# Two rounds of solve products with one stationary operand, merged into 256-column products, and two engines that change banks

## The reference, cut to what matters

```
M = where(stril, einsum("bhncd,bhnmd->bhncm", k_beta, k) * decay, 0.0)
T = solve_triangular(eye + M, eye, lower=True)
v_c = einsum("bhnij,bhnjd->bhnid", T, v_beta)
k_cumdecay = einsum("bhnij,bhnjd->bhnid", T, k_beta * exp(g))
```

## Time and profile before

| | |
|---|---|
| median of three runs | 4081.28 us (4079.53 to 4088.25) |
| the profiled execution | 4083.4 us, span 4081.7 us |
| mean granted TensorE clock | 0.967 |
| TensorE busy | 3375.8 us, 83% |
| VectorE busy | 2804.7 us, 69% |
| ScalarE busy | 1829.1 us, 45% |
| GpSimd busy | 1214.0 us, 30% |

### The profile page before, as it was taken

One profiled execution on the slowest core, in us unless ns is written; L12 is line 12 of the kernel. 1 busy time (PEld: TensorE's weight loads), 2 busy tenths in 40 slices (PEclk: granted clock), 3 DMA queues, 4 the chain that ended last, 5 costly groups with the idle time before them and its releaser, 6 DMA issues. The chain is left out here.

```text
span 4081.7 us, 63279 instructions
## 1 busy us (share of the span) xinstructions
PE 3375.8 (83%) x18978; PEld 2667.9 (65%) x18978; DVE 2804.7 (69%) x5764; ACT 1829.1 (45%) x4272; POOL 1214.0 (30%) x2414
## 2 busy tenths in 40 slices
PE   0000379999999999999999999999999999999987
PEld 0000367777777777777777777777777777777763
DVE  6999357676777767676767676767676766767653
ACT  2222145454545554454545454545454554445541
POOL 2222323233232323232323232332333232323210
PEclk9999989999999999999999999999999999999998
DMA  2000412222222222222222221222222221222202
GB/s 88 0 0 0 188 49 65 76 65 71 68 71 61 69 67 55 69 70 71 70 69 70 65 70 50 70 71 65 73 67 70 64 66 50 71 71 71 65 5 93
DMA packets 288110, 262.37 MB, mean 64 GB/s; under 512 B 220896, under 2 KB 249696, under 8 KB 276960
## 3 DMA queue, kind: packets, MB, share of 16 engines
q1 hardware_dynamic: 278528, 123.60, 12.5%
q10 hardware_dynamic: 9216, 134.22, 8.9%
HBM read 228.11 MB, written 29.62 MB: 63 GB/s over the span
## 5 line engine op out<-in xcount | busy, mean ns | idle before, releaser
L575 PE MATMUL x<-xs,w_high 128*128 128x512 f32 x3072 | 1090.2, 437 | 113.0 <-issue 72.3
L575 PEld LDWEIGHTS x<-xs,w_high 128*128 128x128 f32 x3072 | 546.5, 198 | 182.4 <-issue 79.6
L575 PE MATMUL x<-xs,w_low 128*128 128x512 f32 x1536 | 623.9, 406 | 0.0
L810 ACT ACTIVATE uvec<-rb,cpos 128x128 f32<-128x128 f32 x512 | 160.6, 365 | 957.6 <-PE rb L595 957.6
L869 ACT ACTIVATE slot<-lane 128x512 fp32r<-128x512 f32 x640 | 352.7, 609 | 492.7 <-PE lane L701 492.5
L1149 POOL TENSOR_TENSOR block_step<-block_in 64x14 f32<-64x14 f32 (+6 forms) x896 | 228.6, 255 | 497.0 <-DMA block_in<-blocks_dram 377.3
L1179 POOL TENSOR_TENSOR rstd<-rarg,powers 128x8 f32<-128x8 f32 x64 | 105.0, 1640 | 889.0 <-DVE rarg L988 889.0
L366 PE MATMUL gate<-wba,mixed 128*128 128x64 f32 x128 | 27.6, 421 | 413.1 <-DVE nega L328 413.1
L575 PEld LDWEIGHTS x<-xs,w_low 128*128 128x128 f32 x1536 | 300.1, 195 | 70.9
L940 DVE SCALAR_TENSOR_TENSOR cacc<-x,cwqk,cacc 128x511 f32<-128x511 f32 (+2 forms) x384 | 281.3, 746 | 44.0 <-ACT cacc L797 22.8
L940 DVE SCALAR_TENSOR_TENSOR cacc<-x,cwv,cacc 128x511 f32<-128x511 f32 (+2 forms) x384 | 281.8, 748 | 38.6 <-ACT cacc L797 4.2
(11 more groups left out here) (203 smaller groups left out, 7491.5 us busy)
## 6 DMA issues: line engine op xcount, KB each, us to landing
xs<-mix_dram ACTq DMA_DIRECT2D x64, 2048.0 KB, 7.6
gb<-cum_dram SPq DMA_DIRECT2D x128, 256.0 KB, 4.3
w_in<-in_w_qkvz SPq DMA_DIRECT2D x48, 512.0 KB, 4.9
w_out<-in_w_out SPq DMA_DIRECT2D x16, 512.0 KB, 6.1
blocks_dram<-bt SPq DMA_DIRECT2D x512, 8.0 KB, 1.5
inverse_dram<-block_out SPq DMA_DIRECT2D x64, 128.0 KB, 2.2
inv<-inverse_dram SPq DMA_DIRECT2D x512, 16.0 KB, 1.8
xacc<-in_x SPq DMA_DIRECT2D x1, 4096.0 KB, 13.3
```

Source lines behind the costliest of these rows:

```text
L575: ins = mm(PROJ_BANK[kind][i][:, :], w, x, start=(k == 0 and j == 0), stop=(k == KC - 1 and j == 2))
L810: ins = a(uvec[:, h, :], rb[:, sl(h, HD)], ACT.Copy, scale=sm2[p]["cpos"][:, ch, h:h + 1])
```

## The change

Jobs 3 and 4 no longer go head by head and operand by operand. Job 3 makes, for head 0, the products of s0 with both moving operands, turned and s1, in one piece of 256 columns per chunk; job 4 does the same for head 1. Chunks 0 and 1 go to bank 0, chunks 2 and 3 to bank 1 (`shared_product`). For that, s1 moves into inv16 behind turned, and inv16 changes its order of dimensions. Each bank now holds results for both engines: VectorE takes the turned halves into pinv, ScalarE the s1 halves into lower. VectorE begins with bank 0 and ScalarE with bank 1, and each waits for the other before it takes the other bank. Job 5 waits for both engines. The blocks are stored in two DMAs, one for natural and one for turned, the memset of inv16 covers the new part too, and job 10 takes (s2, pinv) in place of (s1, s2).

```diff
-        inv16 = sb("inv16", [P, HPG, NCH, 2, CH], F32R)
+        inv16 = sb("inv16", [P, 3, HPG, NCH, CH], F32R)
-        slot = [sb(f"slot{i}", [P, HPG, NCH, CH], F32R) for i in range(3)]
+        slot = [sb(f"slot{i}", [P, HPG, NCH, CH], F32R) for i in range(2)]
-        ADDED = (4, 6, 7, 9, 10)
+        COPIED = (0, 1, 2, 3, 4, 5, 8)
+        ADDED = (3, 4, 6, 7, 9, 10)
...
-            if k not in ADDED:
-                engine.wait_ge(copied[h], (JOBS - len(ADDED)) * m + sum(1 for i in range(k + 1) if i not in ADDED))
-            else:
+            if k in COPIED:
+                engine.wait_ge(copied[h], len(COPIED) * m + COPIED.index(k) + 1)
+            if k in ADDED:
                 engine.wait_ge(added[h], len(ADDED) * m + ADDED.index(k) + 1)
...
-                sp.dma_start(t["inverse_dram"].rearrange("a q w i j -> (a q) w i j"), block_out[:, :, :, :].bitcast(F32)).then_inc(S["block_stored"], 16)
-                sp.wait_ge(S["block_stored"], m * 16 + 16)
+                for w in range(2):
+                    sp.dma_start(t["inverse_dram"][:, w].rearrange("a q i j -> a q (i j)"), block_out[:, w, :, :].rearrange("q i j -> q (i j)").bitcast(F32)).then_inc(S["block_stored"], 16)
+                sp.wait_ge(S["block_stored"], m * 32 + 32)
...
             PRODUCTS = [
                 (lower, natural),
                 (natural, lower),
                 (s1, s0),
-                (s0, s1),
-                (s0, turned),
+                None,
+                None,
                 (lower, s2),
                 (s2, pinv),
                 (s0, pinv),
                 (pinv, None),
                 (None, s1),
-                (s1, s2),
+                (s2, pinv),
             ]
+
+            def shared_product(m, k):
+                h = k - 3
+                for half in range(2):
+                    await_product(pe, m, half, k - 1)
+                    for j in range(2):
+                        ch = 2 * half + j
+                        ins = mm(lane[half][:, sl(j, 2 * CH)], s0[:, h, ch, :], inv16[:, 1:3, h, ch, :], start=True, stop=True)
+                    ins.then_inc(prod_full[half], 1)
...
+                if (k, h) == (5, 1):
+                    await_product(pe, m, 0, k - 1)
...
-                        for h in range(HPG):
-                            product(m, n, k - FIRST, h, 1 - p)
+                        if k - FIRST in (3, 4):
+                            shared_product(m, k - FIRST)
+                        else:
+                            for h in range(HPG):
+                                product(m, n, k - FIRST, h, 1 - p)
...
-                    if A and job >= 0 and job not in ADDED:
+                    if A and job in (3, 4):
+                        for half in (1, 0):
+                            act.wait_ge(prod_full[half], JOBS * m + job + 1)
+                            if half == 0:
+                                act.wait_ge(added[0], len(ADDED) * m + ADDED.index(job) + 1)
+                            a(lower[:, job - 3, sl(half, 2), :], lane[half][:, :].rearrange("p (c w s) -> p c w s", c=2, w=2)[:, :, 1, :], ACT.Copy).then_inc(copied[half], 1)
+                    elif A and job in COPIED:
...
-                    if job == 4:
-                        ins = v.tensor_tensor(pinv[:, h, :, :], made, turned[:, h, :, :], ALU.add)
+                    if job in (3, 4):
+                        if h == 1:
+                            dve.wait_ge(copied[1], len(COPIED) * m + COPIED.index(job) + 1)
+                        made = lane[h][:, :].rearrange("p (c w s) -> p c w s", c=2, w=2)[:, :, 0, :]
+                        ins = v.tensor_tensor(pinv[:, job - 3, sl(h, 2), :], made, turned[:, job - 3, sl(h, 2), :], ALU.add)
```

More of the change, by code:

```diff
@@ L520, in scatter_blocks @@
                     rows = slice(a * BLK, (a + 1) * BLK)
-                    sp.dma_start(inv16[rows, :, :, :, rows].rearrange("i h c w j -> i (h c w) j").bitcast(F32),
-                                 t["inverse_dram"][a].rearrange("q w i j -> i (q w) j")).then_inc(S["inv16_loaded"], 16)
+                    sp.dma_start(inv16[rows, 0:2, :, :, rows].rearrange("i w h c j -> i (w h c) j").bitcast(F32),
+                                 t["inverse_dram"][a].rearrange("w q i j -> i (w q) j")).then_inc(S["inv16_loaded"], 16)
             def body(l, m, n, b):
@@ L668, in out_half @@
                     ins.then_inc(S["op_full"], 1)
-            s0, s1, s2 = slot
-            natural, turned = inv16[:, :, :, 0, :], inv16[:, :, :, 1, :]
+            s0, s2 = slot
+            natural, s1 = inv16[:, 0, :, :, :], inv16[:, 2, :, :, :]
             RESIDUAL = JOBS - 2
@@ L909, in body @@
                                 load_input((b + 1) % BATCH)
-            s0, s1, s2 = slot
-            DEST = [s0, s1, s2, lower, pinv, s0, pinv, pinv, s1, s2, solve]
+            s0, s2 = slot
+            s1 = inv16[:, 2, :, :, :]
+            DEST = [s0, s1, s2, None, None, s0, None, None, s1]
             LOOP(act, body)
@@ L919, in _ @@
             W = lambda name, x: dve.wait_ge(S[name], x)
-            s0, s1, s2 = slot
-            turned = inv16[:, :, :, 1, :]
+            s0, s2 = slot
+            turned, s1 = inv16[:, 1, :, :, :], inv16[:, 2, :, :, :]
             def v_columns(m):
@@ L1147, in invert_blocks @@
                     if i == BLK - 2 and m is not None:
-                        pool.wait_ge(S["block_stored"], m * 16 + 16)
+                        pool.wait_ge(S["block_stored"], m * 32 + 32)
                     g.tensor_tensor(step, block_in[:, 0:i, i:i + 1].to_broadcast(shape), block_in[:, i:i + 1, i + 1:BLK].to_broadcast(shape), ALU.mult)
@@ L1318, in build @@
         t["blocks_dram"] = nc.dram_tensor("blocks_dram", [NB, HPG * NCH, BLK, BLK], F32).ap()
-        t["inverse_dram"] = nc.dram_tensor("inverse_dram", [NB, HPG * NCH, 2, BLK, BLK], F32).ap()
+        t["inverse_dram"] = nc.dram_tensor("inverse_dram", [NB, 2, HPG * NCH, BLK, BLK], F32).ap()
         t["later_dram"] = nc.dram_tensor("later_dram", [DIM, TOK], F32).ap()
```

## The result

| | before | after |
|---|---|---|
| time, median (range) | 4083.27 us (4079.53 to 4088.25), 4 runs | 4125.16 us (4121.28 to 4127.31), 4 runs |
| ratio to before, 95% interval | | 1.0101 (1.0083 to 1.0118) |
| span of the profiled execution | 4081.7 us | 4123.1 us |
| mean granted clock | 0.967 | 0.966 |

The change costs 42 us; 104 were forecast, and the range began at 4131. The direction was right, the size was not, and the clock had next to no part in it: the mean granted clock is the same within 0.001.

A forecast was written before the change was run, and what follows sets the result against it. The chain from job 4's additions through L1026 and L1031 to job 7, not TensorE, was taken to bound the stretch. 69 us from its later start plus 35 us of clock, on 4081.3, gave 4185 us; range 4131 to 4240.

The forecast's parts named there:

- The chain that sets the end: From job 4's additions to job 7: L1026 starts 1.10 us later and job 7 with it, 63 x 1.10 = 69 us.
- TensorE's saving: Jobs 3 and 4: wider products take 0.86 us per iteration off TensorE's work, all lost in waits before job 7.
- The order on ScalarE: Per iteration: copies of job 3, table load, exponentials (L829), then copies of job 4, the load and exponentials taking 2.46 us.
- VectorE's wait inside the additions of job 4: VectorE adds bank 1 only after ScalarE's copy of bank 0; L1026 starts 4.77 us after job 3, against 3.67.
- pieces 0.115 us apart: Products of 256 columns in jobs 3 and 4 taken at 0.115 us, between bounds of 0.111 and 0.23.
- The table load: ScalarE, before the exponentials: 1.28 us by the trace, in all 64 iterations.
- the longer switch: The skill's 2.66 us for a table switch with drain; by it the estimate would be 87 us higher; not followed.
- The stores, loads and memset: Two stores delay the loads some 0.5 us, covered by 2.9 us; the larger memset hides behind GpSimd's wait: no cost.
- the copies: ScalarE's copies of 256 columns: 0.477 us for one, 0.84 us for two together, 0.36 us apart.
- the clock: Clock falls during jobs 5 and 6 in half of the iterations: 35 us, between bounds of 0 and 82 us.
- the size of the wait: TensorE before job 5: a new wait of 1.88 us for both engines' emptying of job 4.
- no clock cost: Rival: everything else as forecast, but the short gaps leave the clock alone: 4081 + 69 = 4150 us; chance 0.27.

The follow-up runs named there:

- Pad2: The changed kernel with two more short ScalarE copies, read by nobody, between the exponentials and the copies of job 4: 4203.0 us, 1.0300 of before.
- exp_behind: The changed kernel with the exponentials, and so their table load, moved behind ScalarE's copies of job 4: 4196.9 us, 1.0289 of before.
- narrow: The changed kernel with pieces of 128 columns again, 16 instead of 8 in jobs 3 and 4: 4166.0 us, 1.0211 of before.

## Why the prediction was right in direction and wrong in size

**Right.** The chain that sets the end was as forecast (additions of job 4, masked product, L1031, additions of job 6, job 7), with 4.61 us from the masked product to job 7 and 4.62 measured. TensorE's saving is lost in waits: job 5 now waits for ScalarE, and the iteration still got longer. The order on ScalarE and VectorE's wait inside the additions of job 4 were as forecast. So were the sizes: pieces 0.115 us apart (0.116 to 0.118 by the median, but for the first two of job 4, which the output product ahead of them holds apart), an addition of 256 columns in 0.42 us (0.424). The table load took 1.28 us, by the trace and not the longer switch. The stores, loads and memset cost nothing, as forecast: in the first iteration the loads are issued by 550.3 and job 0 starts at 554.74 without a wait for them:

```profile
543.64 1.36 SPq L514 DMA_DIRECT2D inverse_dram<-block_out  x2
546.56 3.77 SPq L523 DMA_DIRECT2D inv<-inverse_dram  x8
...
554.74 1.09 PE L714 MATMUL lane<-inv,lower 128*128 128x128 f32 x8
```

**Wrong, first: the copies.** The term was "Two copies of 256 columns take 0.84 us together, one 0.477: they follow 0.36 us apart", from L852, which has a factor per partition. Those of the change have none, and last

```profile
L886 ACT ACTIVATE lower<-lane x256: 362/377/391, 564.5 to 3991.3; 128x256 fp32r<-128x256 f32 x128
```

0.377 us, a pair 0.64 to 0.66 (0.27 apart). Both pairs lie on the path. Job 3's copies end 1.36 us behind the start of job 3 and not 1.54; job 4's, started at 3.72 instead of 3.91, end at 4.36 instead of 4.74. So the masked product comes at 4.45 and not at 4.77 us, 0.77 us later than before instead of 1.10: 48 us instead of 69. The mechanism was right, the row chosen for the price was of another form.

**Wrong, second: the clock, 35 us of the sum.** "I take half of the iterations": behind the first iteration neither the kernel after nor the kernel before has a fall during jobs 5 to 7. (Half of the 82 us would have been 41; the 35 follow from nothing that is written there.) The step that failed is the size of the wait. I took 1.88 us; 1.17 was recorded (1.11 in the iteration above). Job 5 came 0.31 us sooner, by the cheaper copies, and TensorE's last output product ended 0.46 us later (3.37 us behind job 3 and not 2.91), mostly since the one behind job 3 had itself to wait 0.32 us for ScalarE's gate. Pad2 has the wait I had in mind, 1.92 us, and there the clock did fall, in nearly every iteration. With the right wait I would still have had no row for it between 1.00 us without a fall and more; the rival "no clock cost" was what happened, and with 4150 it was 25 us above the result: 21 by the copies again, the rest by the end of the kernel. The range began at 4131 because it allowed for copies up to 0.3 us cheaper; on the path they were 0.33 cheaper, and the end of the kernel wasn't in it.

**The end of the kernel** wasn't in the sum: 4.6 us less behind the last job 3, of which only 0.26 us come from the merge. The rest is the clock of the last turns, full in the kernel after where it was low in the kernel before; why isn't known. That it helped the kernel after is luck, as is that the falls behind the key sums (31 against 25, 5.8 us) and the shorter turns (7.1 us) cancel out.

**Not seen at all**, though the rows showed them: the short instructions of VectorE as a second link between the two engines (only exp_behind made it cost something), and the 3.20 us of L1031, which I took as a fixed price of eight instructions. The "TensorE busy throughout" of the forecast holds for the stretch that it names; ahead of job 1 of such an iteration TensorE does wait 0.55 us.

## What to carry to other kernels

Before two engines share the emptying of banks in turns, write down what each has between its two turns: a table load and exponentials beside the path become part of it, and the products saved are worth nothing unless the wait behind them ends sooner. Price an instruction by a row of the same form, operands and scale included. Where a group's mean lies well above its median (474 against 347 ns), look for the engine whose instruction ends where the long ones end: here moving one wait of GpSimd brought 1.6%, some 64 us, more than the 63 x 0.86 = 54 us that the merge takes off TensorE's work.

## What the runs showed of the hardware

- **A VectorE instruction with both inputs in SBUF waited until a GpSimd instruction was over.** One of eight L1031 took up to 1409 ns instead of 347 when GpSimd's L1137 started and ended 0.15 us behind it, in all 64 iterations; 60 of the L951 did so behind L1164 or L1166, up to 2470 ns. The additions L1047, one of whose inputs is in PSUM, ran beside L1137 with at most 692 ns, as without it. With GpSimd's wait moved no L1031 took over 354 ns, and L1137, at most 1491 ns before, took at most 1288. What it is that they contend for wasn't tried.
- **The clock falls behind one-column products with no wait just ahead**, in 13 to 52 of the iterations, by what stands around them. One group of three 512-column pieces ahead of them, on an otherwise equal kernel, took the falls from 52 to 13 and the time from 0.9834 to 0.9710 of before (the two were measured on separate occasions, each against its own runs of before). Why narrow has 44, exp_behind 52 and after 31 isn't settled: the length of the iteration changes in all of them.
- **A wait of 1.17 us on average among products of 128 columns left the clock alone, 1.58 us brought it down in some two thirds of the iterations and 1.92 us in nearly all.**
- **A ScalarE copy of 256 columns** takes 377 ns without a factor (L886) and 477 with one (L852).
- **The table load** took 1.28 us in every kernel, with the exponential 0.01 us behind it. The Trainium skill (ScalarE: Activation LUTs, "What ACT_TABLE_LOAD costs") gives about 2.66 us for a switch with its drain, of which the load itself is 1283 ns. The load agrees; no run here shows the drain.
